# Norm roots, a maximum's product and the feed-forward norm placed on other engines and operands, with a new table of places, in a 6-layer local-attention stack

## The reference

```python
x = x + _layernorm(attn_ref(_layernorm(x)))          # causal, 16 heads, exp replaced by a Taylor map
y = _layernorm(x)
for i in range(6):
    # local attention: 16 heads of 64, window 32, looks one window back
    q, k, v = split(shift_tokens(y) @ Wqkv[i])
    q = q / max(norm(q), 1e-12) * q_scale ; k = k / max(norm(k), 1e-12) * k_scale
    q, k = rotary(q), rotary(k)
    y = softmax(q k^T * 8 + mask) v @ Wo[i] + y
    # feed-forward: layer norm, two matrices, exact gelu gate
    xn = (s - mean(s)) / sqrt(var(s) + 1e-05) * g + bln      # s = shift_tokens(y)
    a, gate = split(xn @ W1 + b1)
    y = a * gelu(gate) @ W2 + b2 + y
x = x + _layernorm(y)
```

## Time and profile before

| | us |
|---|---|
| median of three runs | 3551.12 |
| profiled execution, span | 3553.3 |
| PE busy | 3325.9 (94%) |
| DVE busy | 2737.3 (77%) |
| ACT busy | 2545.5 (72%) |
| POOL busy | 2041.5 (57%) |

### The profile page before, as it was taken

How to read it: one execution, slowest core, us unless ns; L and a number is a source line. 1 busy time by engine, 2 the same in 40 slices (tenths; PEclk the granted TensorE clock), 3 DMA queues, 4 the chain that set the end, 5 groups by cost and what they waited for, 6 DMA issues and landing times.

```text
span 3553.3 us, 149054 instructions
## 1 busy us (share of the span) xinstructions
PE 3325.9 (94%) x65032; PEld 2107.6 (59%) x65032; DVE 2737.3 (77%) x3420; ACT 2545.5 (72%) x5866; POOL 2041.5 (57%) x1557
## 2 busy tenths in 40 slices
PE   7999987999999999999999999999999999999996
PEld 3444434666666666666666666666666666666663
DVE  3656557888887878888788878788888878788883
ACT  4667655777777777777777767677777777787774
POOL 0000006766676666766666666667676667676661
PEclk9999998999999999999999999999999999999998
DMA  3223224333333333433333333334333333333330
GB/s 109 76 71 84 75 61 141 135 127 127 134 133 133 118 127 130 140 131 129 119 122 136 130 124 127 127 124 143 126 130 126 121 136 125 135 127 131 129 122 24
DMA packets 247337, 423.34 MB, mean 119 GB/s; under 512 B 71966, under 2 KB 110108, under 8 KB 246556
## 3 DMA queue, kind: packets, MB, share of 16 engines
q1 hardware_dynamic: 220368, 397.28, 33.1%
q10 hardware_dynamic: 26316, 16.52, 1.6%
HBM read 124.21 MB, written 7.34 MB: 37 GB/s over the span
## 4 chain that ended last, share of the span: by engine, by line
PE 64%; DVE 17%; issue 7%; ACT 5%; POOL 5%; DMA 1%; SPq 1%; DVEq 0%; POOLq 0%; ACTq 0%
PE PS L535 64%; DVE TPB L932 5%; DVE MX L956 2%; ACT SC L1237 1%; DVE NV L947 1%; POOL K L1324 1%; POOL Q L1342 1%; DMA RB<-root_scratch 1%; POOL K L1342 1%; DVE PP L977 1%; DVE PX L978 1%; DVE NV L945 1%; DVE H L800 1%; DVE H L1000 1%; DVE NV L949 1%
## 5 line engine op out<-in xcount | busy, mean ns | idle before, releaser
L932 DVE SCALAR_TENSOR_TENSOR TPB<-PS,VEC,C 128x1024 f32<-128x1024 f32 x768 | 961.8, 1270 | 102.0 <-ACT SX L1213 95.0
L1237 ACT ACTIVATE SC<-PS,BQ,RQ 128x64 f32<-128x64 f32 x3072 | 979.5, 436 | 40.7 <-DVE BQ L961 40.3
L1213 ACT ACTIVATE SX<-PS 128x512 f32<-128x512 f32 x768 | 461.5, 620 | 391.4 <-PE PS L535 388.4
L1324 POOL TENSOR_TENSOR K<-K,RB 128x512 f32<-128x512 f32 x384 | 497.2, 1295 | 283.1 <-DMA RB<-root_scratch 278.4
L1347 POOL TENSOR_TENSOR SC<-SC,RC 128x1024 f32<-128x1024 f32 x192 | 366.3, 1908 | 480.2 <-DVE RC L969 478.8
L535 PEld LDWEIGHTS PS<-PP,VV 32*64 32x64 f32 x24576 | 433.7, 133 | 278.6 <-issue 276.3
L535 PE MATMUL PS<-PP,VV 32*64 32x64 f32 (+1 forms) x24576 | 541.2, 223 | 7.8 <-issue 6.2
L1342 POOL TENSOR_TENSOR K<-TPB,TR 128x512 f32<-128x512 f32 x384 | 496.4, 1293 | 0.0
L1342 POOL TENSOR_TENSOR Q<-TPB,TR 128x512 f32<-128x512 f32 x384 | 495.5, 1290 | 0.0
L535 PE MATMUL PS<-LXH,LH 128*128 128x512 f32 x768 | 371.3, 484 | 85.2 <-DVE TPB L932 68.4
L535 PE MATMUL PS<-K,Q 64*32 64x64 f32 (+1 forms) x24576 | 302.2, 224 | 49.5 <-issue 48.0
(11 more groups left out here) (167 smaller groups left out, 5809.8 us busy)
## 6 DMA issues: line engine op xcount, KB each, us to landing
TR<-TPB SPq DMA_DIRECT2D x768, 256.0 KB, 2.7
RB<-root_scratch SPq DMA_DIRECT2D x768, 128.0 KB
PP<-PX SPq DMA_DIRECT2D x192, 192.0 KB, 2.6
WS<-in_wqkv ACTq DMA_DIRECT2D x72, 128.0 KB, 2.4
PP<-PX SPq DMA_DIRECT2D x192, 48.0 KB, 2.5
QA<-TH SPq DMA_DIRECT2D x128, 64.0 KB, 2.1
QA<-TL SPq DMA_DIRECT2D x128, 64.0 KB, 2.1
KA<-TH SPq DMA_DIRECT2D x128, 64.0 KB, 2.1
```

Source lines behind the costliest of these rows:

```text
L932: e.scalar_tensor_tensor(TPB[:, n % 3:4 + n % 2:3 + n % 2 - n % 3, w, :], g, VEC[:, l, 9 + w:10 + w], C[:, at:at + 1024].rearrange("p (o c ...
L1213: e.activation(SX[i % 3][:, :], bk("PJ", key)[:, :], ACT.Square).then_inc(sem["pj_act"], 1)
L1237: p = e.activation(SC[m % 2][:, g, :, :].rearrange("p x k -> p (x k)"), bank[s][:, at:at + 64], ACT.Exp, bias=BQ[m % 2][:, g:g + 1], scale ...
L1324: e.tensor_tensor(dst, dst, RB[n % 2][:, :], ALU.mult).then_inc(sem["pr_pool"], 1)
```

## The change

- `NM2` goes from DVE (three instructions) to POOL (four: GpSimd does it with plain products and a multiply-add), with its own semaphore `nm_pool`.
- `BQ` becomes a step of its own on POOL. `MX` makes the negated maximum, so `BQ` is one product. S3 waits for `bq_pool` instead of `s1_dve`.
- In the Newton steps of the layer norms and of F2n the intermediate results are written into the PSUM bank of the variance; F2n's result stays there too, and F3 reads it there. The buffers `FX` and `EZ` go. The bank is therefore held longer: until the third Newton instruction for the layer norms, until F3 for the feed-forward norm (before: until the first).
- `PLACE` has new numbers throughout, and a place for `BQ`.

The core of the diff; of `PLACE` the lines with `TB`, `NM2` and `F3`:

```diff
-    "XS": -9.372, "XSl": -9.254, "VP": -0.635, "VC": -0.652, "WO": (12.673, 12.742, 12.742, 12.755),
-    "F1": 13.883, "F2": 14.320, "F2n": 14.625, "F3": 15.347, "F3l": 15.073, "TB": (15.924, 16.229),
+    "WO": (12.583, 12.648, 12.722, 12.753), "F1": 13.519, "F2": 14.269, "F2n": 14.585, "F3": 14.630, "F3l": 14.912,
+    "TB": (16.007, 19.915), "F4": (16.055, 16.097, 16.250), "F5": 16.958, "E1": 18.005,
...
-        lay(z + P["F2"], group, "F2", u, "f2_dve", 3 * u + 1)
+        lay(z + P["F2"], group, "F2", u, "f3_dve", u + 1)
...
-            def rsqrt(v, u, x, step, done, r):
+            def rsqrt(v, x, y, step, done, r):
                 on.wait_ge(step, 2 * r + 2)
-                e.scalar_tensor_tensor(u, v, EPS, x, ALU.add, ALU.mult).then_inc(sem[done], 1)
+                e.scalar_tensor_tensor(v, v, EPS, x, ALU.add, ALU.mult).then_inc(sem[done], 1)
                 on.wait_ge(done, 3 * r + 1)
-                e.scalar_tensor_tensor(u, u, -0.5, x, ALU.mult, ALU.mult).then_inc(sem[done], 1)
+                e.scalar_tensor_tensor(v, v, -0.5, x, ALU.mult, ALU.mult).then_inc(sem[done], 1)
                 on.wait_ge(done, 3 * r + 2)
-                e.scalar_tensor_tensor(x, u, 1.5, x, ALU.add, ALU.mult).then_inc(sem[done], 1)
+                e.scalar_tensor_tensor(y, v, 1.5, x, ALU.add, ALU.mult).then_inc(sem[done], 1)
...
-                    rsqrt(bk("F2", key)[:, :], H[0][:, :], FX[:, :], "f2_act", "f2_dve", u)
+                    rsqrt(bk("F2", key)[:, :], H[0][:, :], bk("F2", key)[:, :], "f2_act", "f2_dve", u)
...
-                e.tensor_reduce(MX[:, :], g, AX_X, ALU.max).then_inc(sem["s1_dve"], 1)
...
-                    e.scalar_tensor_tensor(BQ[m % 2][:, :], MX[:, :], -1.0, rq(m), ALU.mult, ALU.mult).then_inc(sem["s1_dve"], 1)
+                    e.tensor_reduce(MX[:, :], g, AX_X, ALU.max, negate=True).then_inc(sem["s1_dve"], 1)
...
+                elif st == "NM2":
+                    q, = key
+                    v, u, x = NV[:, 0, :], NV[:, 1, :], NV[:, 2, :]
+                    on.wait_ge("nm_act", 2 * q + 2)
+                    e.tensor_tensor(u, v, x, ALU.mult).then_inc(sem["nm_pool"], 1)
+                    on.wait_ge("nm_pool", 4 * q + 1)
+                    e.tensor_tensor(u, u, x, ALU.mult).then_inc(sem["nm_pool"], 1)
+                    on.wait_ge("nm_pool", 4 * q + 2)
+                    e.tensor_scalar(u, u, -0.5, 1.5, ALU.mult, ALU.add).then_inc(sem["nm_pool"], 1)
+                    on.wait_ge("nm_pool", 4 * q + 3)
+                    e.tensor_tensor(x, u, x, ALU.mult).then_inc(sem["nm_pool"], 1)
+                elif st == "BQ":
+                    m, = key
+                    if m > 1:
+                        on.wait_ge("s3_act", 4 * m - 4)
+                    on.wait_ge("rq_act", m // 2 + 1)
+                    on.wait_ge("s1_dve", m + 1)
+                    e.tensor_tensor(BQ[m % 2][:, :], MX[:, :], rq(m), ALU.mult).then_inc(sem["bq_pool"], 1)
```

More of the change, by code:

```diff
@@ L159, in squares @@
     def squares(kind, b):
-        o.put("N2", kind, b, banks=[(None, kind + "_root", 3, 1)])
-        o.keep(o.bank["N2", (kind, b), 0], kind + "_root", 3 * b + 1)
+        o.put("N2", kind, b, banks=[(None, kind + "_root", 3, 3)])
+        o.keep(o.bank["N2", (kind, b), 0], kind + "_root", 3 * b + 3)
     def norm(kind, b, z, places, at=at):
@@ L290, in order @@
             m = n // 2
-            for st in ("S1", "MX", "SU", "NP", "TT", "PX", "PVn"):
+            for st in ("S1", "MX", "BQ", "SU", "NP", "TT", "PX", "PVn"):
                 lay(n + P[st], o.put, st, m)
@@ L427, in nroot @@
         def nroot(kind):
-            return EZ if kind == "end" else NZ[("in", "mid", "x").index(kind)]
+            return ES if kind == "end" else NZ[("in", "mid", "x").index(kind)]
         def nused(kind, b):
@@ L937, in vector_program @@
                     if q:
[L938 removed]
+                        on.wait_ge("nm_pool", 4 * q)
                     on.wait_ge("ss_pe", 8 * q + 8)
                     e.tensor_scalar(NV[:, 0, :], nb[:, 0:128], 1e-24, None, ALU.max).then_inc(sem["nm_dve"], 1)
[L941 to L949 removed]
                 elif st == "MX":
```

38 lines of the change are left out of this document (13 added, 25 removed), and 18 rows, old and new, of the table PLACE.

## The result

| | before | after |
|---|---|---|
| median (4 runs each) | 3552.22 us | **3671.78 us** |
| profiled execution, span | 3553.3 us | 3668.0 us |
| granted TensorE clock over the span | 0.984 | 0.969 |

The changed kernel is slower: its ratio to the kernel before is 1.0337, with an interval of 1.0323 to 1.0352. The forecast of 3649 us is 23 us low, and its range held. The times and ratios here leave out one execution, the profiled one of experiment 10, whose clock was far lower than in all others (4132.85 us at 0.718). What follows shows that the chain of three table loads is the cause, as forecast; that the stretch on which I worked the sum out grew by less than I said, and the clock of TensorE, which my sum doesn't have, made up for it; and that the table loads hide a gain which is larger than I thought.

A forecast was written before the change was run, and what follows sets the result against it. The prediction took PE as the bound, most often held up by DVE. Terms 87 + 24 - 14 - 5 + 6 = +98 us on the 3553.3 us span gave 3651, or 3649 us for the median; range 3570 to 3735.

The forecast's parts named there:

- ACT's chain of three loads: Feed-forward stretch: three table loads of 1.28 us on ACT make exp and S3.3 end 3.5 and 3.8 us later.
- First or second path: Feed-forward stretch: next masks late by +1.55 us through the bank behind the second PT, or small matmuls +1.65 through POOL.
- the new waits of the small matmuls: Sign that the forecast is right: PE's small K,Q matmuls newly wait for POOL's K; no size given.
- NM2 on POOL: Feed-forward stretch: four POOL instructions on 128 columns take 2.0 us with the hops, bounds 1.0 and 3.0.
- The term of +1.9 us a stretch: Feed-forward stretches: POOL's late PR delays S1's small matmuls; 46 x 1.9 = +87 us, bounds +14 to +133.
- The norm stretch: Variance's bank held until F3: 48 x 0.5 = +24 us; fewer waits for PTs: -14 us; bounds -22 to +35.
- issue: PE's waits for "issue", 65.0 us over the kernel before, claimed to be touched by no edit.
- The rest: Elsewhere in the kernel: PE's waits for PT, some 10 us, halve: -5 us.
- The output norms: Eight pairs of loads there, plus first-part norms holding banks 1.4 us longer: +6 us, between 0 and +20.
- DVE's load: Whole kernel: DVE's busy time falls by more than 147 us for BQ plus 75.7 us for L947.
- the loads are hidden: Faster rival: ACT's three loads run while it waits for PE anyway; about 3490 to 3530 us, chance 0.08.
- Dearer switches: Slower rival: each ACT table switch costs twice as much, 175 us on top, about 3825 us; chance 0.03.

The follow-up runs named there:

- experiment 10: Changed kernel with the old PLACE table, except the change's places for BQ and NM2 and F3 right behind F2n; ratio 1.0141 to before, median 3603.0 us.
- the first experiment: Changed kernel with only TB's second place put back (16.260 for 19.915), so 97 table loads again; 3493.92 us, ratio 0.9841 to before.
- experiment 3: Changed kernel with TB's second place at 16.580, between S3.0 and the ln, so two loads in place of three; 3565.25 us, ratio 1.0034 to before.
- experiment 12: The kernel of the first experiment with PV's third part placed earlier (4.700), in the norm stretch only; 3479.31 us, ratio 0.9786 to before.

## Why the prediction was right, step by step

- **ACT's chain of three loads**: right. Laid over the stretch of 803.08, which starts 1.08 us later than that of before, my times put the end of the exp at 817.28, the second PT at 819.13 and the masks at 822.83. Measured: 817.00, 818.70 and 822.40. ACT's instructions overlap by some 0.1 us each, which I had not taken off everywhere.
- **First or second path**: I let POOL's path set the term (+1.65), with the bank's 0.1 us behind it. In the stretch shown the masks come at 822.40 by the bank, and the small matmuls at 822.76, as soon as POOL's PR has ended (822.71); behind masks alone they would start at about 822.6. So the two are within 0.2 us, and the bank has the larger part: PE waited for TPB 60 times (104.8 us), for POOL's K 8 times (9.6 us). Of those 8, 4 lie ahead of the 38 units, so the new waits of the small matmuls that I had named as a sign hardly came. The choice was wrong, at no cost. But the stretch shown grew by only 1.13 us, for my 1.65 by POOL and 1.55 by the bank.
- **NM2 on POOL**: 457, 454, 298 and 455 ns, 1.66 us and 1.9 with the hops (817.08 to 818.98), for my 2.0. BQ: 222 ns for 0.25.
- **The term of +1.9 us a stretch**: measured +1.74 (20.20 for 18.46), but that it came so near is luck in good part. The stretch shown, all at full clock, is only 1.13 us longer than before, and the 12 of the 38 without a piece at half clock are 19.46 us in the mean, +1.00. The other 26 hold such a piece behind the wait and are 20.54 us: 1.08 more, so 0.74 of the 1.74. This is the part I didn't see. The first experiment shows the other: without the loads this stretch would be 17.26 us, 1.20 below before. I had read a gain of 0.69 there, the wait, and treated it as covered, so the comparison with before came out right while the loads' own price was 2.94 us a stretch, and 178 us in all for my 87 + 6.
- **The norm stretch**: sum of +24 and -14, +0.21 us a stretch; measured +0.30. PE's wait for the bank is 1.31 us in the mean (60.4 / 46), for my 1.0. Right in place, low by 0.3: the waits for the bank rose by 46 us (14.5 to 60.4), twice my +24, and those for TPB, 19.0 us in the 38 norm stretches before, are gone altogether.
- **Two terms that the sum lacks**: the time at half clock rose from 114.7 to 227.6 us, worth +56 us, and the waits for "issue" fell from 65.0 to 24.5 us, -40. I had left the clock out, and of "issue" (waits for which the profile names no other engine) I had said that no edit touches it. That the one takes back most of the other is luck. With the waits for TPB (+36), for the bank (+46) and for ES (+11) they come to +108, near the 114.7 us between the spans.
- **The rest**: the short and the long stretch together -0.15 us a unit, 38 times: -6 us, for my -5. The number came out, the reason didn't: I had put it down to waits for PT, and what fell there are the waits for "issue", from 41 to 13 us in the 38 units.
- **The output norms**: this term was mis-sized. The last layer grew by 44.9 us. 7.75 units at 1.88 us are 14.6 of it, so some 30 us are its own, where I put +6 with a bound of +20. Six of the eight pairs of loads of L1002 and L1004 (2.57 us a pair) fall into its short stretches, the other two into the tail. The first seven short stretches are 15.45 us in the mean, for 13.03, and in five of them PE waits some 2 us for ES (10.8 us in all), a wait that the first experiment doesn't have. And the clock is lower, 0.94 for 1.00 in the windows, 58.0 us at half clock for 3.4:

```profile
2999.70:3478.30 478.60, 453.53 (x10052) 299.98 (x10052) 391.10 (x468) 365.68 (x873) 317.81 (x235) 1.00 0.37 125
```

```profile
3064.70:3588.20 523.50, 474.45 (x10044) 311.31 (x10043) 338.28 (x395) 411.76 (x908) 340.28 (x325) 0.94 0.34 115
```

  (the first row is of before, the second of after; the columns are the window, its length, the busy time of PE, PEld, DVE, ACT and POOL, the granted clock, DMA's share and GB/s).
- **DVE's load**: down by 324.9 us, more than the 222.7 I named. By the groups of before, BQ held 133.2 us (192 x 693 ns; I had multiplied the median, 768) and NM2's three instructions 185.4. No time came of it while the loads stood, as said.
- **PE's busy time**: I said unchanged. It grew by 40.8 us (3366.7 for 3325.9), because a matmul at half clock is busy for longer.
- **The rivals**: "the loads are hidden" fell, by the 2.15 us wait. Its number for the gain without loads, 3490 to 3530, was that of the first experiment, 3494, though not by its sum: there the waits for TPB fell by 63 us, those for the bank rose by 46, and those for "issue" fell by 35. Dearer switches fell too: the ln starts at 815.07 behind a load that begins at 813.77 and lasts 1.28. The drain of about 1.38 us that the Trainium skill (ScalarE: Activation LUTs, "What ACT_TABLE_LOAD costs") adds to each switch shows in no row here. Nor does this program get the single load for ln and then exp that the Trainium skill has (ScalarE: Activation LUTs, "Table sets: the hidden batching unit"), unless a load of its own (TB's) stands ahead of both: experiment 3 has no load between them, the changed kernel has one.

## What to carry to other kernels

Before a table load is moved past other steps, list every function that the engine runs until it, in order: each change of set there is a load of its own on that path, and three in a row moved a whole chain here. An edit that takes work from a full engine is to be judged together with what it makes the other engine wait for: BQ on POOL is +1.5% alone in the old order, and its absence is +3% in the new. And a wait of the bounding engine is worth more than its length if the clock falls behind it, so the first thing to fill is the longest single wait, in the one stretch where it stands; and the stretch behind it is to be measured too, since more than half of what experiment 12 gained in one it lost in the next.
